# Reordering the end of attention and the routing in a one-core cross-attention and expert kernel, with filler matmuls ahead of the experts

## The chip, the cores and the metric

The kernel runs on one core of one Trainium2 chip. The metric is the device time of one execution in microseconds (us). A change of about 1% (2.3 us) is what a measurement of this kernel can tell from no change.

## What is computed

The reference is two blocks on x (1024 rows of 128) and a context of 6404 rows of 128. Cut to what matters:

```python
def xattn(c, q, ...):                         # c = layernorm(x), q = context
    cq = einsum('bcd,bqd,d->bcq', c, q, w_cq) + b_cq
    s = (c @ w_c + b_c)[:, :, None] + (q @ w_q + b_q)[:, None, :] + cq
    a = softmax(s, axis=2);  c2q = einsum('bcq,bqd->bcd', a, q)
    b_att = softmax(max(s, axis=2), axis=1)
    q2c = einsum('bc,bcd->bd', b_att, c)[:, None, :]
    return concat([c, c2q, c * c2q, c * q2c]) @ W_l.T + b_l
def ffn(x, ...):                              # 8 experts, one chosen per row by argmax
    expert_id = argmax(x @ wr + br)
    return gelu(x @ w1[e] + b1[e]) @ w2[e] + b2[e]    # e = expert_id of the row
x = x + xattn(layernorm(x), ctx, ...)
x = x + ffn(layernorm(x), ...)
```

## The kernel before

The 1024 rows are 8 tiles of 128 (t = 0 to 7); T = 8, TA = 7, H = 4. The context is cut into 7 pieces of up to 1024 (NG = 7; the last has 260 columns, three tiles). For each row tile TensorE makes the scores, VectorE (DVE) takes them out of PSUM with their maximum (L798), ScalarE (ACT) does the exponential (L649) and its rounded float16 part (L664), and DVE (`low`, L815) or, for a few pieces, GpSimd (POOL, L531) makes the float16 remainder. SyncE (SP) then transposes each piece by DMA, strictly in order of pieces (L391), and TensorE's `weighted(t, e)` (L1073, L1075) multiplies the transposed piece e of tile t with the context. In the last tile (t = 7) POOL makes the remainders of pieces 1, 3 and 5, DVE those of 0, 2, 4 and 6.

Behind the last scores there is a long tail with an order written out by hand on each engine; an engine takes its own instructions in order, and waits are semaphores:

- `attended(t)` (DVE, L820 to L828) divides the sums of tile t by the softmax total; it waits for the last `weighted(t, 6)`. `turn_a(g)` (TensorE, L1117) transposes the result of a group of tiles, `transposed(g)` (DVE, L870, L871) copies it out and multiplies it by c.
- `mean_context` (TensorE, L1174, L1176) makes q2c; DVE turns it into the weights `wc2` (L899 to L902).
- `linear_a(g)` (L1132, L1134) and `linear_c(g)` (L1141) are the output linear layer; `residual(g)` (DVE, L879) adds x; `statistics`, `variance`, `deviation` are the second layernorm, with one square root on ACT (L620); x2n is its result (L916 on DVE for tiles 0 to 3, L681 on ACT for tiles 4 to 6).
- Tiles 0 to 6 are dispatched: `turn_x2` (TensorE, L1153), `router` (L1160, L1166), `best` (DVE, L928 to L933), the one-hot choice (L939, `chosen_ready`), the ranks (TensorE, L1210 to L1217), the position arithmetic (DVE, L945 to L955, `pos_ready`). POOL then scatters the 7 tiles of rows into DRAM (L600), and SP reads them back sorted by expert in batches (L447). SP has filled that DRAM area with empty rows before (L429).
- The last tile (7) is not dispatched: it goes through all 8 experts as blocks 0 to 7, with a mask. Its chain is `residual(2)`, `statistics`, `normalise`, a transpose (L1221), its copies (L690, L964), then the first `up`.
- The experts are 22 blocks: 8 for the last tile, 14 of dispatched rows. `up(b)` (L1265 to L1268) makes the hidden layer, `down(b)` (L1279 to L1285) the output; a loop runs `up(b + 2)` before `down(b)`. At b = 6 and later `turn(g)` (L1239) transposes the batches of sorted rows. `up(8)` waits for `xT_low` of the first batch (DVE L975, behind an ACT copy). POOL scatters each block to the output (L606).

Of the kernel before, what the change touches and what calls it, by code (L numbers as in the profile page):

```python
# [30 lines left out]
P = 128  # L31


def build(nc, x, ctxT, w3, b3, wlT, b_l, wr, br, w1, b1, w2, b2, out):
# [45 lines left out]
    with es:  # L80
# [637 lines left out]
        def _(dve):  # L718
# [98 lines left out]
            def attended(t):  # L817

                acc = psA[t % 2]
                nc.vector.tensor_reduce(out=Ls[:, :], in_=Lp[:, t * NG:(t + 1) * NG], axis=AX.X,  # L820
                                        op=ALU.add).then_inc(o_small, 1)
                dve.wait_ge(o_small, 3 * t + 1)
                nc.vector.reciprocal(Li[:, :], Ls[:, :]).then_inc(o_small, 1)
                dve.wait_ge(o_small, 3 * t + 2)
                dve.wait_ge(pv_done, (t + 1) * NG)
                nc.vector.tensor_scalar(otmp[:, :], acc[:, 0:D], Li[:, :], None, ALU.mult).then_inc(o_small, 1)
                dve.wait_ge(o_small, 3 * t + 3)
                nc.vector.scalar_tensor_tensor(out=a_sb[:, t * D:(t + 1) * D], in0=acc[:, D:2 * D],  # L828
                                               scalar=Li[:, :], in1=otmp[:, :], op0=ALU.mult,
                                               op1=ALU.add).then_inc(o_out, 1)  # L830
# [42 lines left out]
            def residual(g):  # L873
# [21 lines left out]
            transposed(1)  # L895
            attended(T - 2)

# [5 lines left out]
                                           op0=ALU.mult, op1=ALU.add).then_inc(wc2_ready, 1)  # L903
            low(T - 1, 4)
            transposed(2)
            residual(0)
            low(T - 1, 6)
            statistics(x1, 0, H)
            residual(1)
            statistics(x1, H, TA)  # L910
            variance(0, TA)
            deviation(0, TA)
# [5 lines left out]
            attended(T - 1)  # L918
            transposed(3)

# [19 lines left out]

            residual(2)
            statistics(x1, TA, T)

# [11 lines left out]
            nc.vector.tensor_copy(pos[:, :], posf[:, :]).then_inc(pos_ready, 1)  # L955

            normalise(x1, x2n, TA, T, x2n_ready)

# [69 lines left out]
        def _(pe):  # L1028
# [141 lines left out]
            def mean_context():  # L1170

                pe.wait_ge(eb_ready, 1)
                for t in range(T):
# [3 lines left out]
                    .then_inc(q2c_in_psum, 1)  # L1177

            weighted(T - 2, 2)
            pe.wait_ge(scores_out, T * NG)  # L1180
# [7 lines left out]
                .then_inc(top_in_psum, 1)  # L1188
            weighted(T - 2, 4)
            weighted(T - 2, 5)  # L1190
            linear_a(0)
            weighted(T - 2, 6)
            mean_context()
            linear_a(1)
            weighted(T - 1, 0)
            turn_a(2)
            linear_c(0)
            weighted(T - 1, 1)
            linear_a(2)
            linear_c(1)  # L1200
            for e in range(2, NG):
                weighted(T - 1, e)
            turn_x2()
            turn_a(3)
            router()
            linear_a(3)
            linear_c(2)

# [7 lines left out]
            for t in range(TA):  # L1216
                last = nc.tensor.matmul(count_psum, ones16[:, :], oneh[:, t, :], start=(t == 0), stop=(t == TA - 1))  # L1217
            last.then_inc(ranks_in_psum, 1)

            pe.wait_ge(x2n_ready, H + 1)  # L1220
# [75 lines left out]
            for b in range(NBLK):  # L1296
                if b == E - 2:
                    turn(0)
                for g, (s0, _) in enumerate(BATCHES):
                    if g >= 2 and b == E + s0 - 5:  # L1300
                        turn(g)
                if b + 2 < NBLK:
                    up(b + 2)
                if b == E - 2:
                    turn(1)
                down(b)

# [30 lines left out]
```

## Time and profile before

| | us |
|---|---|
| median of 3 runs | 233.35 |
| the runs | 233.14, 234.91, 233.35 |
| the profiled execution's time | 234.7 |
| its span in the trace | 233.0 |

Busy shares of the span: TensorE 86%, DVE 77%, ACT 68%, POOL 54%. Stages of the profiled span: attention up to about 150 us, the tail of attention with the routing up to 181.4 us, the experts up to about 227 us, and the last scatters of the output. The profiled execution's own time is 1.7 us over its span, and 1.35 us over the median of the runs.

### The profile page before, as it was taken

What the parts mean: (1) busy time and instruction counts of PE and PEld (TensorE: products, weight loads), DVE (VectorE), ACT (ScalarE), POOL (GpSimd) and SP (SyncE); (2) the same over time, 40 slices, a digit from 0 to 9 for tenths busy, and PEclk for the clock granted to TensorE, in tenths of its full rate; (3) what the DMA queues carried; (4) which work ended last, traced back from release to release, by engine and by line L of the source; (5) the groups of instructions that cost most, each with busy time, mean ns of one, the idle gap of its engine ahead of it and who ended that gap; (6) DMA issues with size and microseconds to landing.
All of it is one profiled execution on the core that took longest, in us unless ns stands there. A gap on an engine that the chain in (4) does not pass through costs nothing.

```text
span 233.0 us, 5011 instructions
## 1 busy us (share of the span) xinstructions
PE 200.8 (86%) x1837; PEld 151.4 (65%) x1837; DVE 180.4 (77%) x395; ACT 157.9 (68%) x249; POOL 126.6 (54%) x177
## 2 busy tenths in 40 slices
PE   0289969999999999979989999899992899799970
PEld 0133436776866777746656777699981899789960
DVE  2999797697998997997995999957848437567770
ACT  2752899399399698699596799789332355766630
POOL 3695819708906808958608957655302730027783
PEclk9999985799999999999999999999996569999995
DMA  6999979979999999999989999989991559999100
GB/s 208 381 259 258 221 239 249 225 192 191 232 180 227 260 220 271 231 200 240 230 207 274 207 249 230 211 180 212 234 284 47 191 191 314 366 370 344 43 21 0
DMA packets 142958, 51.78 MB, mean 222 GB/s; under 512 B 121172, under 2 KB 140773, under 8 KB 142934
## 3 DMA queue, kind: packets, MB, share of 16 engines
q1 hardware_dynamic: 142000, 50.08, 92.8%
q0 software_dynamic: 784, 1.38, 1.7%
q8 instruction: 14, 0.23, 0.4%
q14 instruction: 10, 0.08, 0.1%
q10 hardware_dynamic: 150, 0.00, 0.0%
HBM read 10.74 MB, written 3.75 MB: 62 GB/s over the span
## 4 chain that ended last, share of the span: by engine, by line
PE 41%; DVE 23%; issue 13%; DMA 11%; POOL 6%; ACT 4%; SPq 1%; POOLq 0%; DVEq 0%; ACTq 0%
DMA PT<-Phl 9%; DVE S L798 6%; PE psX L1073 6%; PE psS L1055 5%; PE psS L1053 5%; PE psS L1054 5%; POOL out_x L606 5%; PE psO L1073 4%; DVE Phl L815 4%; PE psX L1075 3%; ACT S L649 3%; PE psO L1075 2%; PE psS L1279 2%; DMA S<-in_x 2%; PE psX L1084 2%
## 5 line engine op out<-in xcount | busy, mean ns | idle before, releaser
L649 ACT ACTIVATE S<-S,negb 128x1024 f32<-128x1024 f32 x48 | 55.0, 1145 | 17.5 <-DVE negb L806 17.5
L798 DVE TENSOR_SCALAR_CACHE_REDUCE S<-psS 128x1024 f32<-128x1024 f32 x48 | 58.2, 1216 | 9.9 <-PE psS L1055 9.8
L815 DVE TENSOR_TENSOR Phl<-S,Phl 128x1024 f16<-128x1024 f32 x38 | 51.5, 1354 | 5.3 <-ACT Phl L664 5.2
L531 POOL TENSOR_TENSOR Phl<-S,Phl 128x256 f16<-128x256 f32 x40 | 26.4, 691 | 52.2 <-ACT Phl L664 52.2
L664 ACT CAST Phl<-S 128x1024 f16<-128x1024 f32 x48 | 50.2, 1045 | 5.6 <-DMA PT<-Phl 4.2
L1053 PE MATMUL psS<-qT,gh 128*128 128x512 f16 x96 | 37.6, 392 | 5.6 <-DVE gl L776 3.0
L1073 PE MATMUL psO<-qn,PT 128*128 128x256 f16 x204 | 37.7, 279 | 0.7 <-DMA PT<-Phl 0.7
L1073 PE MATMUL psX<-qn,PT 128*128 128x256 f16 x204 | 36.4, 273 | 2.0 <-DMA PT<-Phl 2.0
L1055 PE MATMUL psS<-qT,gl 128*128 128x512 f16 x96 | 37.7, 393 | 0.0
L1054 PE MATMUL psS<-qT,gh 128*128 128x512 f16 x96 | 37.7, 393 | 0.0
L1075 PE MATMUL psO<-qn,PT 128*128 128x128 f16 x204 | 36.2, 223 | 0.0
L1075 PE MATMUL psX<-qn,PT 128*128 128x128 f16 x204 | 35.0, 219 | 0.0
L606 POOL DMA_INDIRECT out_x<-stageT,S x14 | 16.8, 1198 | 24.3 <-DVE stageT L1006 18.5
L1073 PEld LDWEIGHTS psO<-qn,PT 128*128 128x128 f16 x204 | 20.4, 100 | 6.5 <-DMA PT<-Phl 1.9
L1073 PEld LDWEIGHTS psX<-qn,PT 128*128 128x128 f16 x204 | 20.0, 98 | 6.7 <-DMA PT<-Phl 2.7
L708 ACT ACTIVATE Phl<-psS 128x512 f16<-128x512 f32 x22 | 13.1, 597 | 15.4 <-PE psS L1268 8.7
L1075 PEld LDWEIGHTS psO<-qn,PT 128*128 128x128 f16 x204 | 20.4, 100 | 2.2 <-issue 0.3
L1075 PEld LDWEIGHTS psX<-qn,PT 128*128 128x128 f16 x204 | 20.0, 98 | 2.1
L1053 PEld LDWEIGHTS psS<-qT,gh 128*128 128x128 f16 x96 | 9.8, 102 | 14.7 <-DVE S L798 3.5
L1055 PEld LDWEIGHTS psS<-qT,gl 128*128 128x128 f16 x96 | 9.7, 101 | 12.1 <-issue 1.4
L983 DVE TENSOR_TENSOR Phl<-Phl 128x512 f16<-128x512 f32 x22 | 15.0, 681 | 2.4 <-issue 2.4
L572 POOL TENSOR_TENSOR wp<-stageT,wp 128x256 f16<-128x256 f32 x16 | 15.2, 982 | 0.3
(239 smaller groups left out, 426.3 us busy)
## 6 DMA issues: line engine op xcount, KB each, us to landing
PT<-wp SPq DMA_DIRECT2D x8, 512.0 KB, 6.0
stageT<-in_ctxT SPq DMA_DIRECT2D x6, 512.0 KB, 7.3
qn<-wp SPq DMA_DIRECT2D x6, 512.0 KB, 6.5
wp<-in_w SPq DMA_DIRECT2D x4, 512.0 KB, 4.8
stageT<-in_w SPq DMA_DIRECT2D x4, 512.0 KB, 4.8
rows_by_expert<-stageT SPq DMA_DIRECT2D x4, 385.5 KB, 5.3
PT<-Phl SPq DMA_TRANSPOSE x48, 4.2
S<-rows_by_expert SPq DMA_DIRECT2D x2, 258.0 KB, 5.9
```

The lines of the kernel that those rows point to most:

```text
L531: last = nc.gpsimd.tensor_tensor(lo[:, r], slot(t, e)[:, r], hi[:, r], ALU.subtract)
L572: last = nc.gpsimd.tensor_tensor(parts[:, 1, at + a:at + a + CHUNK], src[:, a:a + CHUNK], parts[:, 0, at + a:at + a + CHUNK], ALU.subtract)
L606: pool.indirect_dma_start(out=out, out_offset=bass.IndirectOffsetOnAxis(ap=rows[:, b, 2 * D:ROW].bitcast(I32), axis=0), in_=yf[:, b, :], i ...
L649: nc.scalar.activation(slot(t, e), slot(t, e), ACT.Exp, bias=negb[:, t:t + 1], accum_out=Lp[:, t * NG + e:t * NG + e + 1]).then_inc(exp_do ...
L664: nc.scalar.copy(hi, slot(t, e)).then_inc(high_done, 1)
L798: nc.vector.tensor_scalar(out=into, in0=bank(u, n)[:, 0:into.shape[1]], scalar1=1.0 / GS, scalar2=None, op0=ALU.mult, op1=ALU.max, accum_o ...
L815: nc.vector.tensor_tensor(lo, slot(t, e), hi, ALU.subtract).then_inc(low_done, 1)
L1053: nc.tensor.matmul(dst, g_h, hi, start=True, stop=False)
L1054: nc.tensor.matmul(dst, g_h, lo, start=False, stop=False)
L1055: last = nc.tensor.matmul(dst, g_l, hi, start=False, stop=True)
L1073: nc.tensor.matmul(acc[:, 0:2 * D].rearrange("p (a d) -> p a d", a=2), PT[:, 2 * e * TW + i, :], both[:, :, i, :], start=(j == 0), stop=Fa ...
L1075: last = nc.tensor.matmul(acc[:, 0:D], PT[:, 2 * e * TW + n + i, :], both[:, 0, i, :], start=False, stop=(j == QT - 1), skip_group_check=True)
```

## The change

On DVE, `attended(6)` goes behind `wc2`; the remainders `low(7, 4)` and `low(7, 6)` go behind the statistics of the first and second group; `transposed(3)` goes from before `best` to behind the one-hot choice; `residual(2)` and the statistics of the last tile go from before the ranks to behind the positions. On TensorE the pieces of `weighted`, the linear layer and the transposes are put in another order: `turn_x2` and `router` stand ahead of the last one or two pieces of tile 7, `linear_a(3)` and `linear_c(2)` behind the ranks, and then 12 new matmuls over constant ones, 512 columns each, run whose result nobody reads (`fill(12)`). At expert block 6, `down(6)` goes ahead of `up(8)`.

```diff
--- before.py
+++ after.py
@@ -893,7 +893,6 @@
             nc.vector.tensor_scalar(nM[:, :], psS[0][:, CH:CH + 1], -1.0, None, ALU.mult).then_inc(nM_ready, 1)
             low(T - 1, 2)
             transposed(1)
-            attended(T - 2)
 
             dve.wait_ge(q2c_in_psum, 1)
             link(nc.vector.reciprocal(Bi[:, :], psS[1][:, CH:CH + 1]))
@@ -901,13 +900,14 @@
             dve.wait_ge(late_landed, 16 * NLATE)
             nc.vector.scalar_tensor_tensor(out=wc2[:, :], in0=wl[:, 3, :], scalar=q2c[:, :], in1=wl[:, 0, :],
                                            op0=ALU.mult, op1=ALU.add).then_inc(wc2_ready, 1)
-            low(T - 1, 4)
+            attended(T - 2)
             transposed(2)
             residual(0)
-            low(T - 1, 6)
             statistics(x1, 0, H)
+            low(T - 1, 4)
             residual(1)
             statistics(x1, H, TA)
+            low(T - 1, 6)
             variance(0, TA)
             deviation(0, TA)
             nc.vector.scalar_tensor_tensor(out=sc1[:, H:TA], in0=mv[:, H:TA, 0], scalar=-1.0, in1=rstd[:, H:TA],
@@ -916,7 +916,6 @@
                 nc.vector.tensor_scalar(x2n[:, t, :], x1[:, t, :], mv[:, t, 0:1], rstd[:, t:t + 1],
                                         ALU.subtract, ALU.mult).then_inc(x2n_ready, 1)
             attended(T - 1)
-            transposed(3)
 
             iob = iota_e[:, :].unsqueeze(1)
 
@@ -938,8 +937,7 @@
             io, first = best(router_psum, 0, TA)
             nc.vector.tensor_tensor(oneh[:, :, :], io, first, ALU.is_equal).then_inc(chosen_ready, 1)
 
-            residual(2)
-            statistics(x1, TA, T)
+            transposed(3)
 
             dve.wait_ge(ranks_in_psum, 1)
             link(nc.vector.tensor_tensor(more[:, :, :], count_psum.unsqueeze(2).broadcast_to([P, E, TA]),
@@ -954,6 +952,8 @@
             link(nc.vector.tensor_reduce(out=posf[:, :], in_=rank[:, :, :], axis=AX.X, op=ALU.add))
             nc.vector.tensor_copy(pos[:, :], posf[:, :]).then_inc(pos_ready, 1)
 
+            residual(2)
+            statistics(x1, TA, T)
             normalise(x1, x2n, TA, T, x2n_ready)
 
             link(nc.vector.scalar_tensor_tensor(out=eblk[:, :], in0=nblk[:, :], scalar=float(P), in1=sblk[:, :],
@@ -1176,6 +1176,14 @@
                 nc.tensor.matmul(psS[1][:, CH:CH + 1], ones[:, :], es1[:, :], start=True, stop=True)\
                     .then_inc(q2c_in_psum, 1)
 
+            filler = ones[:, :].bitcast(F16)
+
+            def fill(n):
+
+                for _ in range(n):
+                    nc.tensor.matmul(psS[2][:, 0:CH], filler[:, 0:P],
+                                     filler.unsqueeze(1).broadcast_to([P, 2, 2 * P]), start=True, stop=True)
+
             weighted(T - 2, 2)
             pe.wait_ge(scores_out, T * NG)
             turn_a(0)
@@ -1187,24 +1195,23 @@
             nc.tensor.matmul(psS[0][:, CH:CH + 1], ones[0:1, :], m2[:, :], start=True, stop=True)\
                 .then_inc(top_in_psum, 1)
             weighted(T - 2, 4)
+            linear_a(0)
             weighted(T - 2, 5)
-            linear_a(0)
+            mean_context()
             weighted(T - 2, 6)
-            mean_context()
             linear_a(1)
+            linear_c(0)
+            turn_a(2)
             weighted(T - 1, 0)
-            turn_a(2)
-            linear_c(0)
-            weighted(T - 1, 1)
             linear_a(2)
             linear_c(1)
-            for e in range(2, NG):
+            for e in range(1, NG - 2):
                 weighted(T - 1, e)
             turn_x2()
+            weighted(T - 1, NG - 2)
+            router()
+            weighted(T - 1, NG - 1)
             turn_a(3)
-            router()
-            linear_a(3)
-            linear_c(2)
 
             pe.wait_ge(chosen_ready, 1)
             nc.tensor.matmul(rank_psum, before[:, :], oneh[:, :, :].rearrange("p t e -> p (t e)"),
@@ -1216,6 +1223,10 @@
             for t in range(TA):
                 last = nc.tensor.matmul(count_psum, ones16[:, :], oneh[:, t, :], start=(t == 0), stop=(t == TA - 1))
             last.then_inc(ranks_in_psum, 1)
+
+            linear_a(3)
+            linear_c(2)
+            fill(12)
 
             pe.wait_ge(x2n_ready, H + 1)
             nc.tensor.transpose(x7T_psum, x2n[:, TA, :], idf[:, :]).then_inc(x7T_in_psum, 1)
@@ -1296,6 +1307,7 @@
             for b in range(NBLK):
                 if b == E - 2:
                     turn(0)
+                    down(b)
                 for g, (s0, _) in enumerate(BATCHES):
                     if g >= 2 and b == E + s0 - 5:
                         turn(g)
@@ -1303,7 +1315,8 @@
                     up(b + 2)
                 if b == E - 2:
                     turn(1)
-                down(b)
+                else:
+                    down(b)
 
 
 def kernel(**inputs):
```

## Rows read from the trace of the kernel before

**Rows 1.** Windows view, late stages: each engine's busy us, TensorE's granted clock, DMA

```profile
176.50:180.00 3.50, 0.00 (x0) 0.00 (x0) 2.82 (x16) 1.46 (x2) 0.66 (x1) 0.50 0.02 7
181.40:190.10 8.70, 8.66 (x72) 8.22 (x73) 2.59 (x12) 3.02 (x7) 5.60 (x6) 0.50 0.60 214
190.20:197.50 7.30, 7.30 (x115) 7.07 (x113) 5.40 (x14) 4.68 (x9) 0.00 (x0) 1.00 0.88 260
```

**Rows 2.** Timeline, TensorE: start, length in us, [idle before <- releaser]

```profile
156.97 1.90 PE L1174 MATMUL psS<-eb,c_sb 128*128 128x1 f32 x16
...
169.16 0.28 PE L1073 MATMUL psX<-qn,PT 128*128 128x256 f16 x1 [0.30 <-DMA PT<-Phl]
...
170.99 0.93 PE L1153 MATMUL psS<-idf,qT 128*128 128x128 f32 x7
...
172.67 1.73 PE L1166 MATMUL psS<-wrs,S 128*128 128x8 f32 x14
```

**Rows 3.** Timeline of DVE from the last tile's remainders to x2n

```profile
155.68 1.22 DVE L815 TENSOR_TENSOR Phl<-S,Phl 128x1024 f16<-128x1024 f32 x1 [2.67 <-ACT Phl L664]
...
157.61 0.15 DVE L820 TENSOR_REDUCE Ls<-Lp 128x1 f32<-128x7 f32 x1
...
158.38 0.35 DVE L828 SCALAR_TENSOR_TENSOR a_sb<-psO,Li,otmp 128x128 f32<-128x128 f32 x1
...
159.52 0.51 DVE L902 SCALAR_TENSOR_TENSOR gh<-wl,q2c 128x128 f32<-128x128 f32 x1
160.12 1.52 DVE L815 TENSOR_TENSOR Phl<-S,Phl 128x1024 f16<-128x1024 f32 x1
...
162.86 0.69 DVE L879 TENSOR_TENSOR qT<-psS,stageT 128x512 f32<-128x512 f32 x1 [0.61 <-PE psS L1141]
...
166.90 0.17 DVE L741 TENSOR_SCALAR sc<-mv 128x7 f32<-128x7 f32 x1
...
168.47 1.11 DVE L916 TENSOR_SCALAR qT<-qT,mv,rstd 128x128 f32<-128x128 f32 x4
```

**Rows 4.** SyncE's queue at the transpose of piece 5 of the last tile

```profile
165.20 1.63 SPq L391 DMA_TRANSPOSE PT<-Phl  x1
```

**Rows 5.** DMA view of that one issue: the last number is us to landing

```profile
PT<-Phl SPq DMA_TRANSPOSE x1, 3.9
```

**Rows 6.** Timeline of DVE from the router to the last tile's layernorm

```profile
174.50 0.22 DVE L928 TENSOR_REDUCE S<-psS 128x7 f32<-128x56 f32 x1 [1.40 <-PE psS L1166]
...
175.50 0.22 DVE L939 TENSOR_TENSOR S<-iota_e,S 128x56 f16<-128x56 f32 x1
175.63 0.28 DVE L879 TENSOR_TENSOR qT<-psO,stageT 128x128 f32<-128x128 f32 x1
...
176.28 0.18 DVE L735 BATCH_NORM_AGGREGATE mv<-st 128x2 f32<-128x6 f32 x1
176.50 0.22 DVE L945 TENSOR_TENSOR S<-psS,kedge 128x56 f32<-128x56 f32 x1
...
178.34 0.14 DVE L741 TENSOR_SCALAR sc<-mv 128x1 f32<-128x1 f32 x1
...
179.72 0.35 DVE L760 TENSOR_SCALAR qT<-qT,mv,rstd 128x128 f32<-128x128 f32 x1
```

**Rows 7.** Timeline of TensorE in the experts: first up, first waiting up, one down

```profile
181.44 0.27 PE L1265 MATMUL psS<-S,wp 128*128 128x128 f16 x1 [0.84 <-DVE S L964]
...
199.51 0.23 PE L1265 MATMUL psS<-S,PT 128*128 128x128 f16 x1 [1.44 <-DVE S L975]
...
200.86 0.60 PE L1279 MATMUL psS<-wp,Phl 128*128 128x256 f16 x4
...
201.57 0.22 PE L1265 MATMUL psS<-S,PT 128*128 128x128 f16 x1
```

**Rows 8.** SyncE's queue: first read-back of sorted rows

```profile
190.01 0.90 SPq L447 DMA_DIRECT2D S<-rows_by_expert  x2
```

**Rows 9.** DMA view of the first of these two issues

```profile
S<-rows_by_expert SPq DMA_DIRECT2D x1, 192.0 KB, 2.6
```

## The prediction, made before the changed kernel was run

> **What bounds the kernel now.** I read the page first: TensorE is busy 86% of the span and the granted clock is at half only in two stretches, one early and one around the start of the experts. The change touches nothing before about 151 us, so I took the windows view of the late stages, and then the timelines of TensorE and DVE through them. Three things are to be seen.
>
> First, the end of attention. TensorE waits 0.30 us for a DMA transpose at 169.16, ahead of the last two pieces of tile 7; then come the x2n transposes at 170.99 and the router matmuls, done at 174.4 [rows 2]. DVE had x2n for tiles 0 to 3 ready at 168.47 + 1.11 = 169.58 [rows 3], so `turn_x2` stood 1.4 us behind `weighted`. That is all that the new order can win there.
>
> Second, the routing. `best` starts at 174.50, the choice at 175.50, the positions at 176.50, and these end as the variance of tile 7 starts, 178.34; tile 7 is normalised at 180.07 [rows 6], and the first `up` starts at 181.44 [rows 7]. This is a chain of short DVE operations, and TensorE idles in it: none busy from 176.5 to 180 [rows 1].
>
> Third, the experts. After that idle stretch the granted clock is 0.50, which is 1.2 GHz, from 181.4 to 190.1, with TensorE busy 8.66 of 8.70 us; from 190.2 to 197.5 it is 1.00, 2.4 GHz, busy all the time [rows 1]. So the experts are bound by TensorE, and the half clock costs 8.7 / 2 = 4.35 us. There is one stall: `up(8)` waits 1.44 us [rows 7].
>
> **The change, part by part.**
>
> *(a) x2n.* In `mean_context` 0.50 us of `weighted(6, 6)` are moved behind it, so it starts 156.97 - 0.5 [rows 2] and `wc2`, done at 160.03, comes 0.5 to 0.6 us earlier. But DVE's work up to the variance at 166.90 gains `attended(6)`, 158.73 - 157.61 = 1.12 us, which now lies in DVE's wait for q2c, and which moves behind `wc2`. The idle 0.61 us before `residual(0)` [rows 3] goes; about 0.5 us comes back, because `turn_a(2)` now waits on TensorE behind `linear_c(0)` and DVE waits for it. The sum is -0.55 + 1.12 - 0.61 + 0.5 = +0.46: x2n is ready at about 170.0 in place of 169.6. Bounds: -0.3 (no new wait, and a shorter `low`) and +0.9.
>
> *(b) Piece 4 of tile 7.* `low(7, 4)` ran at 160.12 to 161.64. It now stands behind `residual(0)` and four tiles' statistics. From the new end of `wc2`, 159.45: `attended(6)` 1.12, the wait for `turn_a(2)` 0.5, `transposed(2)` 0.65, `residual(0)` 0.7, and the statistics, for which I take 1.3 of the 4.04 us between 162.86 and 166.90 [rows 3] (this stretch holds them with two residuals, `low(7, 6)` and three tiles more); the remainder starts near 163.8 and ends near 165.3. SP issues transposes in order of pieces, and piece 5, whose remainder POOL finishes at 165.2, is queued behind piece 4. One issue takes 1.63 us [rows 4] and lands 3.9 us after its start [rows 5]. So piece 4 lands at 165.3 + 3.9 = 169.2 or, as the two issues are close to each other, a little later, say 169.6; piece 5 at 167.0 + 3.9 = 170.9, where it landed at 169.1. TensorE would be ready for piece 4 near 167.4, so it idles about 2.2 us. That is hidden in part, since x2n isn't ready before 170.0, but `weighted(7, 4)`, eight times 384 columns, ends at 170.9 (a `down` has 1664 columns and takes 0.71 us [rows 7], so 3072 take 1.31 us), and `turn_x2` starts there: the same moment as before, and not 1.4 us earlier. Low bound: if the piece lands by 168.7, `turn_x2` starts with x2n, 0.9 us earlier.
>
> DVE's remainder took 1.22 us at 155.68, when POOL was idle, and 1.52 us at 160.12, beside a POOL remainder [rows 3]. Its new place is beside POOL's last remainder, so I take the longer one. The Trainium skill (SBUF — State Buffer, Who interferes with whom) says that a DVE operation with two SBUF inputs contends with a GpSimd one that reads SBUF; by that rule the move costs both engines. The trace agrees, with the 1.52 against 1.22 us.
>
> *(c) The router and the choice.* `turn_x2` takes 0.9 us, then `weighted(7, 5)` 1.3 us covers the ACT copies of x2T, then the router 2.05 us (two small ones ahead of the 1.73 [rows 2]): 170.9 + 0.85 + 1.32 + 2.05 = 175.1, against 174.4. Now the new wait: on DVE `attended(7)` still stands before `best`, and it needs `weighted(7, 6)`, which is now behind the router: 0.55 us, and then 0.75 us for its two long operations, each like the 0.35 us at 158.38 [rows 3]. `best` starts at 175.1 + 0.6 + 0.8 = 176.55 in place of 174.50: **+2.05 us** for the choice. Behind it are queued the ranks, the positions, POOL's row scatters and SP's read-backs. Bounds: +1.1 (piece 4 in time, x2n not later) and +2.6.
>
> *(d) Behind the choice.* `transposed(3)` (0.6 us) lies under the rank matmuls, whose result set the next step at 176.50 - 175.50 = 1.0 us after the choice; that is 0.1 us shorter at best. `residual(2)` and the statistics, 175.63 to 176.46 = 0.84 us [rows 6], were under the ranks and now are behind the positions, bare. So the first `up` is 5.94 - 0.1 + 0.84 = 6.7 us behind the choice, which starts at 177.55: 184.25 in place of 181.44 [rows 7], **+2.8 us**.
>
> *(e) The filler.* `linear_a(3)` and `linear_c(2)` are 0.7 us at full clock, and twelve matmuls of 512 columns, by a `down`'s 1664 columns in 0.71 us, are 2.6 us; double both at half clock. From the end of the ranks, 178.5, they reach 181.7 at full clock or 185 at half clock; the transpose of x2n, queued behind them, could start at 182.9. I expect the clock to be at half by the ranks, as it was by 176.5 [rows 1], since router, idle and ranks together are longer now. Then the filler is 6.5 us of unbroken work, which like the unbroken work before 190.1 brings the clock back, mostly before the experts start; on the way it delays the first `up` by up to 1 us, 0.25 in the middle. Credit: 4.35 - 0.25 = **-4.1 us**. Bounds: 0 (the clock is at half again or still) and -4.35. The filler writes a bank that no one reads then, and costs nothing else.
>
> That filler is needed is also what the Trainium skill says (TensorE: Matmul & The Clock Gate, Part 1): throttled is the default, activity releases it, and one kernel has different numbers of slow matmuls from execution to execution. By the second half, the 8.7 us of this execution aren't those of every one; the runs, 233.14 to 234.91 about a profiled 234.7, fit that.
>
> *(f) `down(6)` before `up(8)`.* A `down` takes 201.57 - 200.86 = 0.71 us [rows 7]. `up(8)` waits for a DVE operation which this doesn't move, so the whole `down` goes into the 1.44 us stall: **-0.7 us**; 0 if the stall is gone or the rows are late.
>
> The other moves on TensorE (linear and `weighted` pieces changing places, `turn_a(3)`) cost nothing: same instructions, under DVE's chain. From `up(8)` on all is as before, paced by TensorE.
>
> **Sum** on the profiled execution's own 234.7 us: + 2.8 - 4.1 - 0.7 = 232.7. It is 1.35 us over the median; I give the median's difference no part, because most of it lies in the length of the half-clock stretch, which this change replaces; I forecast 232.6 for the median, that is 0.3% below 233.35.
>
> **The rivals.**
>
> 1. *The forecast*: later start, warm clock. 232.6, own range 231.4 to 234.0. Chance 0.50.
>
> 2. *The cold start stays* (other side). The filler ends and about 1.2 us of idle, the transpose and 0.8 us more follow before `up(0)`; or the filler at half clock is too short. For it speaks that it took 8.7 us of nearly unbroken work to bring the clock back at 190.1, more than the filler has; against it, that this work had thin stretches (the router of tile 7 lies in it), and that a filler of 512 columns has none. Then 234.7 + 2.8 - 0.7 = 236.8. It decides from 3.3 us of remaining half-clock cost (over 6.6 us at half clock). Chance 0.16; cases between, with 3 to 6 us at half clock, give 234.2 to 235.7, chance 0.10.
>
> 3. *Attention's end is not late.* Piece 4 lands in time and x2n is no later, so the choice is at +1.1: 232.6 - 0.95 = 231.7; with a warm clock throughout, an unhindered filler and shorter waits, 230.8. For it: my +0.46 and +0.5 are small sums of guesses. Chance 0.19, nearly all of it counted as faster where the experts also gain.
>
> 4. *The rows bind.* The first sorted rows land at 190.01 + 2.6 = 192.6 [rows 8, 9]; all of it goes with the positions, +1.95: 194.6. `turn(0)` stands at 198.07 - 1.6 = 196.5 after the change. So 1.9 us of slack; if scatters or read-backs slow by more than that, the time is about 233.5. Chance 0.05.
>
> **The numbers.** Over 1% faster is under 231.0, over 1% slower over 235.7. Faster: rival 3, 0.19. Slower: rival 2, 0.16. Within 1%: 0.65. Range 230.8 to 235.8: from rival 3's end up to where the cold start decides.
>
> **What would show it.** Right: a TensorE idle before `weighted(7, 4)`, released by a DMA; `best` behind `attended(7)` at about 176.5; the first `up` near 184 to 185; granted clock 1.00 in nearly all of the first eight blocks; no 1.44 us stall before `up(8)` without a `down` in it. Wrong: `up(0)` earlier than 183.5, or a clock of 0.5 for over 4 us behind it, or a wait of `turn(0)` for rows.

## The result, and the profile of the changed kernel

The changed kernel took 237.0 us in the median of 4 runs (236.15 to 237.42), the kernel before 233.78 (233.14 to 234.91): ratio 1.0114, 95% interval 1.0073 to 1.0154. I had forecast 232.6 with a range up to 235.8. It is 1.1% slower, the interval leaves out 1, and the time is outside the range.

The profiled execution of the changed kernel took 236.77 us, its span is 235.04 (233.0 before). Below, times are also given from the start of the DVE operation that makes `nM`, the last thing both kernels do in the same order (L893 in both). Windows view of the changed kernel (engines' busy us, then the granted clock, DMA share, GB/s), which answers to [rows 1]:

```profile
178.00:184.80 6.80, 5.68 (x29) 3.26 (x30) 5.64 (x28) 1.63 (x3) 1.44 (x2) 0.50 0.27 84
186.90:198.90 12.00, 12.00 (x185) 11.60 (x186) 8.00 (x25) 7.64 (x15) 3.87 (x4) 1.00 0.57 194
```

The filler did what it was expected to: the granted clock was 0.50 from 178.0 to 184.8, under the ranks and the filler, and the first blocks ran at 1.00 throughout. Timeline of DVE, which answers to [rows 3] and [rows 6]:

```profile
155.00 0.15 DVE L893 TENSOR_SCALAR nM<-psS 128x1 f32<-128x1 f32 x1
...
165.89 1.65 DVE L815 TENSOR_TENSOR Phl<-S,Phl 128x1024 f16<-128x1024 f32 x1
...
171.01 1.11 DVE L916 TENSOR_SCALAR qT<-qT,mv,rstd 128x128 f32<-128x128 f32 x4
...
177.68 0.35 DVE L826 TENSOR_SCALAR otmp<-psX,Li 128x128 f32<-128x128 f32 x1 [5.30 <-PE psX L1075]
...
179.32 0.22 DVE L938 TENSOR_TENSOR S<-iota_e,S 128x56 f16<-128x56 f32 x1
```

Timeline of POOL, the remainder that runs beside DVE's at 165.89:

```profile
164.53 3.54 POOL L531 TENSOR_TENSOR Phl<-S,Phl 128x256 f16<-128x256 f32 x4 [1.82 <-ACT Phl L664]
```

Timeline of TensorE, which answers to [rows 2] and [rows 7]:

```profile
171.47 0.28 PE L1073 MATMUL psX<-qn,PT 128*128 128x256 f16 x1 [1.81 <-DMA PT<-Phl]
...
172.80 0.93 PE L1153 MATMUL psS<-idf,qT 128*128 128x128 f32 x7
...
181.57 4.37 PE L1184 MATMUL psS<-ones 128*128 128x512 f16 x12
185.77 0.27 PE L1232 MATMUL psO<-idf,qT 128*128 128x128 f32 x1
186.89 0.22 PE L1276 MATMUL psS<-S,wp 128*128 128x128 f16 x1 [0.84 <-DVE S L964]
...
208.89 0.66 PE L1250 MATMUL psX<-idf,S 128*128 128x128 f32 x4 [1.17 <-DMA S<-rows_by_expert]
```

TensorE waits 1.81 us for piece 4's transpose; `attended(7)` (L826) waits for the last piece behind the router, and the choice (L938) is 24.32 us behind `nM`, against 22.64 before; the first `up` is 31.88 us behind it, against 28.58. The last row is new: the third turn of sorted rows (the third `turn(g)`) waits for its DMA. In the kernel before, the same turn waited for nothing:

```profile
206.87 0.61 PE L1239 MATMUL psX<-idf,S 128*128 128x128 f32 x4
```

SP's first read-back, which answers to [rows 8]:

```profile
195.71 0.90 SPq L447 DMA_DIRECT2D S<-rows_by_expert  x2
```

That is 40.7 us behind `nM` in place of 37.15: 3.55 us later. The positions account for 1.6 us of it (done at 27.14 us behind `nM`, 25.57 before), and the scatters' landing for the rest: from the end of POOL's last scatter to the read-back it is 3.82 us here and 1.48 before.

The table holds the eleven profiles that the argument uses most; the names are explained with the experiments.

| us behind `nM` (start of it in the span) | choice | first up | first read-back | third turn | end of span |
|---|---|---|---|---|---|
| before (152.86) | 22.64 | 28.58 | 37.15 | 54.01 | 80.11 |
| before_again (153.16) | 22.63 | 28.57 | 37.79 | 52.48 | 78.59 |
| changed (155.01) | 24.32 | 31.88 | 40.70 | 53.88 | 80.03 |
| after_again (153.02) | 24.25 | 30.84 | 40.01 | 53.69 | 81.48 |
| after_third (154.72) | 24.28 | 30.90 | 39.03 | 56.20 | 82.50 |
| after_nofill (153.65) | 24.24 | 30.92 | 39.12 | 55.28 | 81.39 |
| after_w6_first (153.94) | 23.59 | 31.40 | 39.40 | 54.60 | 82.46 |
| after_low4_w6 (155.95) | 22.16 | 28.85 | 37.15 | 54.15 | 80.54 |
| before_fill (155.07) | 22.57 | 28.36 | 37.57 | 50.96 | 77.11 |
| before_fill_fourth (153.98) | 22.62 | 28.50 | 38.07 | 51.97 | 78.12 |
| before_fill_third (154.16) | 22.73 | 28.76 | 39.23 | 55.08 | 81.19 |

### The profile page after: what moved, and what is told of

It is laid out like the page before. It is cut to its first block, busy times and chain, and to the rows that moved or that the text cites. A ratio compares the mean times of both kernels' runs of the same rounds, so it can differ in the third digit from the quotient of the medians.

```text
span 235.0 us, 5034 instructions
## 1 busy us (share of the span) xinstructions
PE 202.7 (86%) x1849; PEld 149.8 (64%) x1849; DVE 180.1 (77%) x395; ACT 157.7 (67%) x249; POOL 126.9 (54%) x177
## 4 chain that ended last, share of the span: by engine, by line
PE 44%; DVE 20%; DMA 14%; issue 9%; POOL 5%; SPq 4%; ACT 1%; POOLq 0%; DVEq 0%
DMA PT<-Phl 7%; PE psO L1073 6%; PE psS L1053 6%; PE psX L1073 6%; PE psS L1055 6%; PE psS L1054 6%; DVE S L798 6%; DVE Phl L815 6%; DMA S<-rows_by_expert 3%; PE psO L1075 3%; PE psX L1075 3%; POOL rows_by_expert L600 3%; POOL out_x L606 2%; DMA rows_by_expert<-qT,S 2%; DMA S<-in_x 2%
## 5 line engine op out<-in xcount | busy, mean ns | idle before, releaser
L531 POOL TENSOR_TENSOR Phl<-S,Phl 128x256 f16<-128x256 f32 x40 | 27.1, 710 | 51.8 <-ACT Phl L664 51.8
L708 ACT ACTIVATE Phl<-psS 128x512 f16<-128x512 f32 x22 | 13.2, 599 | 10.7 <-PE psS L1279 10.7
L1055 PEld LDWEIGHTS psS<-qT,gl 128*128 128x128 f16 x96 | 9.7, 101 | 12.1 <-issue 1.4
L572 POOL TENSOR_TENSOR wp<-wp 128x256 f16<-128x256 f32 x16 | 15.4, 989 | 0.3
```

The lines of the kernel that those rows point to most:

```text
L531: last = nc.gpsimd.tensor_tensor(lo[:, r], slot(t, e)[:, r], hi[:, r], ALU.subtract)
L572: last = nc.gpsimd.tensor_tensor(parts[:, 1, at + a:at + a + CHUNK], src[:, a:a + CHUNK], parts[:, 0, at + a:at + a + CHUNK], ALU.subtract)
L1055: last = nc.tensor.matmul(dst, g_l, hi, start=False, stop=True)
```

## The experiments

The runs came in five groups. Each group ran on one chip beside the kernel before (the expectations call a group a call); ratios are to the kernel before of the same group, with 95% intervals. The groups' chips differ, and that matters below. Theories of the first group: H, the first 150 us vary by themselves; P, the changed program is slower there; F, the filler earns its 3 to 4 us; R, the sorted rows cap what it earns. Later groups use letters that their expectations explain.

**First group: both kernels again, and the filler taken from one and given to the other.**

> The kernel before, once more, for a second profile of it. Anchor: the start of the DVE operation that makes nM (the end of the untouched head), 152.86 us in the first profile of before and 155.00 us in that of the changed kernel; the rest of the span was 80.1 and 80.0 us. Theory H (the head varies from execution to execution, whatever the program): this profile's anchor lies anywhere from 152.5 to 155.5. Theory P (the changed program has a slower head by itself): the anchor is again 152.5 to 153.3. The rest of the span is 78.5 to 80.1 us by both, shorter where the half-clock stretch at the start of the experts is shorter than the 8.7 us of the first profile. Time ratio 1.000 to within 0.3%.

> The changed kernel, once more. Theory H: its anchor lies anywhere from 152.5 to 155.5 us, and the ratio to before comes from the rest of the span alone, which is then 80.0 us against about 79 us in a typical execution of before: ratio 1.003 to 1.006. Theory P: anchor again 154.5 to 155.5 and ratio about 1.011.

```diff
 after_nofill (from the changed kernel)
-            fill(12)
```

> The changed kernel without the twelve filler matmuls. Theory F (the filler is what brings the clock back before the experts and so earns 3 to 4 us): the first up starts about 1.1 us earlier, but at half clock for 6 to 9 us; the sorted rows bind less. Time 1 to 2.5 us above the changed kernel. Theory R (the sorted rows bind anyway, so a warm start is worth little): the filler gained at most what the rows leave; time within 0.7 us of the changed kernel, on either side.

```diff
 before_fill (from the kernel before; fill as the changed kernel has it)
             last.then_inc(ranks_in_psum, 1)
+            fill(12)
```

> The kernel before with the same twelve filler matmuls behind the ranks and nothing else changed. Theory F: the clock is at full speed for nearly all of the first eight blocks and the time falls by 2.5 to 3.7 us (ratio 0.984 to 0.989), the rest of the 4.35 us going to waits for sorted rows at the third and fourth batch. Theory R: the rows bind from the first batch on, and the time falls by less than 1 us (ratio over 0.996).

Measured: before_again 1.0014 (0.9977 to 1.005); after_again 1.010 (1.0062 to 1.0138); after_nofill 1.011 (1.0058 to 1.0162); before_fill 0.9954 (0.992 to 0.9989).

*The head.* `nM` starts at 153.02 us in after_again, at 153.16 in before_again, at 155.07 in before_fill, whose program is that of before up to there. Over all twenty profiles its mean is 153.9 us, for kernels built from the old order and from the new one alike. So the head goes by theory H: the 2.15 us that the first pair of profiles shows ahead of 155 us (152.86 against 155.01) don't come from the change, though they are the whole difference of that pair. The ratio of 1.010, from 12 runs of the changed kernel beside 29 of the kernel before, is the measure of the change. It is above the 1.003 to 1.006 that I had expected by H: the rest of the kernel loses more than I thought.

*The tail*, from before_again and after_again, the same chip, 78.59 against 81.48 us. (The medians of these two differ by 2.4 us; this pair of executions is somewhat further apart.) Windows of before_again, then of after_again:

```profile
181.80:187.20 5.40, 5.40 (x46) 5.18 (x46) 1.94 (x9) 1.97 (x5) 4.03 (x5) 0.50 0.69 246
```

```profile
183.80:195.90 12.10, 12.04 (x186) 11.68 (x187) 8.05 (x25) 7.70 (x15) 5.02 (x5) 1.00 0.58 193
208.10:211.40 3.30, 3.30 (x29) 2.97 (x27) 1.68 (x4) 1.08 (x2) 0.00 (x0) 0.50 1.09 363
```

Third turn of after_again in TensorE's timeline:

```profile
206.71 0.66 PE L1250 MATMUL psX<-idf,S 128*128 128x128 f32 x4 [2.02 <-DMA S<-rows_by_expert]
```

First up +2.27; from there to the first turn 14.63 against 12.08, -2.55 (this execution of before had 5.6 us at half clock, and not 8.7); first to third turn 9.28 against 10.77, +1.49, which is +2.02 of waiting for rows, -0.72 of `down(6)` and 0.2 of smaller things; from the third turn to the end 26.11 against 27.79, +1.68, which is the half clock from 208.1 to 211.4: TensorE had just waited 2.02 us for the rows. (Waits of 1.17 and 1.92 us there, in the first profile of the changed kernel and in before_fill_fourth below, were not followed by one.) The sum is +2.89 us.

*Where the filler's gain goes.* before_fill starts its first up where before does and has no half clock at all from there; up to the first turn it gains 2.5 us on before_again. At the third turn it waits:

```profile
206.03 0.66 PE L1248 MATMUL psX<-idf,S 128*128 128x128 f32 x4 [1.05 <-DMA S<-rows_by_expert]
```

In the four profiles where that turn waits for rows and SP's order is that of before (changed, after_again, before_fill, before_fill_fourth) it starts 13.2 to 13.9 us behind SP's first read-back, whenever TensorE gets there. before stood 3.6 us above the lowest of these, before_again 1.5. So a warm start is worth about that much and no more, and a later read-back of a kernel that waits there is paid in full. That is R rather than F: the time fell by 0.46%, about 1.1 us, and not by the 1.1 to 1.6% of F. (I had put R's limit at 1 us and the first batch; it is the third that binds.)

And after_nofill, with 7.9 us at half clock, is as fast as the changed kernel (1.011 against 1.010, each to within some 0.5%). Its third turn comes 55.28 us behind `nM` and waits for nothing. With the filler it comes at 53.69 (after_again) and 53.88 (changed), 1.4 to 1.6 us earlier, for the warm start's 3.7 us, and after_again loses even these again to its second half-clock stretch. In the runs the filler buys the changed kernel nothing that can be told from noise.

Windows view of after_nofill:

```profile
184.60:192.50 7.90, 7.90 (x65) 7.43 (x66) 2.28 (x10) 3.38 (x7) 4.63 (x5) 0.50 0.66 233
```

**Second group: single parts.**

```diff
 before_down6: down(6) ahead of up(8), in the kernel before
 after_w6_first (from the changed kernel)
-            router()
             weighted(T - 1, NG - 1)
+            router()
 after_rows_early (from the changed kernel)
+            block_rows(2, 0, D, rows_landed)
             fetch(4)
             fetch(5)
-            block_rows(2, 0, D, rows_landed)
 (and block_rows(3, 0, D, rows_landed) ahead of fetch(8))
 before_fill_down6_rows: filler, down(6) and this order in the kernel before
```

> The kernel before with down(6) ahead of up(8) and nothing else changed. Theory D (TensorE paces the experts from their start): the 0.7 us of the down go into the stall of 1.44 us and the time falls by 0.6 to 0.8 us, ratio 0.997. Theory R (the third batch of sorted rows, turned 13.2 us after SP's first read-back, binds in many executions): in the two profiles of before the third turn stood 3.6 and 1.4 us above that, so by R also the 0.7 us are had, unless the clock comes back early. Ratio 0.997 to 0.999 by R.

> The changed kernel with weighted(7, 6) ahead of the router, so that attended(7) on DVE runs under the router and no longer between the router and best. Theory R: what sets the end is SP's first read-back of sorted rows, which follows the positions. The choice comes 0.6 to 0.8 us earlier, the first read-back too, and the time falls by as much: 0.7 us, ratio to before about 1.007. If the empty rows' landing holds back the scatters instead (theory E: the scatters waited for it in three profiles), the choice comes earlier but the first scatter doesn't, and the time stays within 0.3 us of the changed kernel.

> The changed kernel with SP's read-back of the third and fourth batch of rows moved ahead of two and one weight fetches. Theory R: the third turn no longer waits (1.2 and 2.0 us in the two profiles of the changed kernel), the clock doesn't fall a second time, and the time falls by 1.2 to 2.5 us, ratio to before 1.000 to 1.005. Theory D (the rows' wait is only where the engine would lose the time anyway, at a later block's weights): less than 0.5 us.

> The kernel before with the filler, down(6) ahead of up(8), and the earlier read-back of the third and fourth batch. Theory R: the filler's warm start, worth 0.46% alone, is no longer capped by the rows: the first up to the third turn takes 21.3 us (22.6 with the filler alone), time 2.3 to 3.3 us under before, ratio 0.986 to 0.990. Theory D: the weights of the dispatched blocks bind instead, ratio 0.993 to 0.996.

Measured: 0.9998 (0.9955 to 1.004), 1.006 (1.0016 to 1.0104), 1.013 (1.0085 to 1.0176), 1.0063 (1.0026 to 1.01).

before_down6: its own part is seen in the trace, first to third turn 8.57 us in place of 9.29; the run's time can't tell 0.3%. after_w6_first: the choice is 0.7 us earlier, as expected. Its ratio points the same way, but the changed kernel itself did not run on this chip and the intervals overlap, so the gain in time isn't shown. The last two were clear misses. No turn waits for rows (after_rows_early's third stands at 208.12 with no wait), but TensorE got there late, because of gaps that no engine releases; so these two don't test whether earlier rows lift R's cap. after_w6_first has such gaps too. None of the six profiles of the first pair and the first group has them. before_fill shows them when it is run again in later groups; timeline of TensorE in before_fill_third:

```profile
187.83 0.22 PE L1277 MATMUL psS<-stageT 128*128 128x128 f16 x1 [0.50 <-issue]
...
188.54 0.22 PE L1275 MATMUL psS<-S,wp 128*128 128x128 f16 x1 [0.43 <-issue]
...
189.27 0.22 PE L1276 MATMUL psS<-S,wp 128*128 128x128 f16 x1 [0.52 <-issue]
...
190.67 0.22 PE L1276 MATMUL psS<-S,wp 128*128 128x128 f16 x1 [1.01 <-issue]
```

Each gap is followed by two to ten weight loads and matmuls and then the next gap; they come to 2.0 to 3.2 us of idle TensorE in all. Windows view of the same stretch, in before_fill_third and then in before_fill, which has none:

```profile
187.00:191.00 4.00, 1.54 (x20) 0.91 (x18) 0.11 (x1) 1.29 (x3) 1.94 (x3) 1.00 0.77 275
```

```profile
187.00:191.00 4.00, 4.00 (x65) 3.88 (x63) 2.70 (x9) 3.04 (x7) 3.39 (x3) 1.00 0.80 286
```

The idle time is not their whole price. In seven of the nine profiles that have them with 12 filler matmuls, the granted clock then falls to half for 3.4 us, as here in before_fill_third:

```profile
191.40:194.80 3.40, 3.28 (x27) 2.74 (x26) 1.92 (x5) 2.00 (x5) 0.00 (x0) 0.50 0.08 10
```

From the first up to the first turn takes 12.1 to 12.2 us in the four profiles with the filler, without gaps and with SP's old order, 14.6 and 14.9 in the two where the clock stays up behind the gaps (after_w6_first, after_rows_early), and 16.7 to 17.8 in the seven where it falls. So the gaps cost 2.5 to 5.7 us, as much as the filler gains there (2.5 and 4.1 us against the two profiles of before) or more.

**Third group: rows or gaps, and the two late steps of the order undone together.**

```diff
 before_fill_again: before_fill once more
 before_fill_rows: before_fill with the rows' order of after_rows_early
 before_fill_late (from before_fill)
-            for b in range(FIRST):
-                fetch(b)
             sp.reg_load(expert_reg[FIRST:NB], bexp[0:1, FIRST:NB])
             ...
             block_rows(0, 0, D, rows_landed)
+            for b in range(FIRST):
+                fetch(b)
             block_rows(1, 0, D, rows_landed)
 after_low4_w6 (from the changed kernel): after_w6_first, and on DVE
             attended(T - 2)
+            low(T - 1, 4)
             transposed(2)
             residual(0)
             statistics(x1, 0, H)
-            low(T - 1, 4)
```

> The kernel before with the filler alone, once more. Theory R: 0.3 to 0.7% under before again (0.46% in the first call), with the third turn waiting about 1 us for its rows. Theory I (TensorE, once it is fast at the start of the experts, runs into gaps of about 1 us that no engine releases, as it did for 2 to 3 us between 185 and 191 us in three of the four profiles of the second call, and in none of the first): where such gaps show in the profile, the gain is less, down to none.

> The kernel before with the filler and with the read-back of the third and fourth batch of rows issued ahead of two and one weight fetches. Theory R: from the first up to the third turn 21.4 us in place of 22.6, no wait of a turn for rows, and 0.8 to 1.2 us under the kernel with the filler alone. Theory W (the reordering takes from the weights what it gives the rows): no more than 0.3 us under it, with waits of up for a fetched weight.

> The kernel before with the filler, and the first two weight fetches (0.5 MB each, which kept the DMA engines full from 185 to 189 us) issued behind the first read-back of rows instead of ahead of the last scatters. Theory I with its cause in these transfers (they delay TensorE's own supply of instructions): no gap of TensorE without a releaser before 190 us, in a call where the other filler kernels show them. Against it: the gaps stay. Either way the first read-back starts 0.5 to 1 us earlier, as the scatters have the DMA engines for themselves, and the third turn moves with what is queued ahead of its rows, 0 to 2 us later.

> The changed kernel with low(7, 4) back ahead of transposed(2) and weighted(7, 6) ahead of the router. By the steps of the prediction the choice was late by what these two cost: piece 4's wait (1.8 us of TensorE idle in the changed kernel, of which about 0.5 to 1 us reach the router) and attended(7) ahead of best (0.75 us). Expected: the choice 22.6 to 23.1 us behind nM (24.3 in the changed kernel, 22.6 before), no DMA wait ahead of piece 4, and the time 1.2 to 1.7 us under the changed kernel, ratio to before 1.002 to 1.005. If the time stays above 1.008, what costs is not the choice but what is behind it (tile 7's statistics behind the positions, and the filler's delay of x2n's transpose).

Measured: 1.0061 (1.0018 to 1.0104), 1.0055 (1.0021 to 1.009), 1.0051 (1.0002 to 1.0101), 1.0048 (1.0014 to 1.0083).

All four profiles have the gaps, 2.5 to 3.2 us, and the half clock behind them. before_fill, 0.46% faster in the first group, is 0.61% slower in this one. The gaps stay in before_fill_late, so the two fetches are not their cause. The rows' order can't be judged while TensorE is late for the third turn anyway.

after_low4_w6 shows what the order had cost at the choice. Its timeline of DVE:

```profile
155.95 0.15 DVE L893 TENSOR_SCALAR nM<-psS 128x1 f32<-128x1 f32 x1
...
163.44 1.28 DVE L815 TENSOR_TENSOR Phl<-S,Phl 128x1024 f16<-128x1024 f32 x1
...
175.11 0.35 DVE L826 TENSOR_SCALAR otmp<-psX,Li 128x128 f32<-128x128 f32 x1 [2.70 <-PE psX L1075]
...
177.11 0.21 DVE L927 TENSOR_REDUCE S<-psS 128x7 f32<-128x56 f32 x1 [1.27 <-PE psS L1166]
...
178.11 0.22 DVE L938 TENSOR_TENSOR S<-iota_e,S 128x56 f16<-128x56 f32 x1
```

`attended(7)` now runs under the router, and `best` waits for the router alone. The choice is 22.16 us behind `nM`: 2.1 us earlier than in the changed kernel and 0.5 earlier than before. The first up comes 2 us earlier than in the changed kernel. With these two undone the new order is no longer a loss: 1.0048 beside 1.0061 for before with the filler, same chip, both with the gaps. The changed kernel as it was did not run in this group, so the gain in time over it, 1.010 to 1.0048, is one across chips.

**Fourth group: is the gap tied to the stream of instructions?**

```diff
 after_third, before_fill_third: the changed kernel and before_fill once more
 before_fill72, after_fill72: 72 filler matmuls of 128 columns for 12 of 512
```

> The changed kernel, a third time, as the control of this call: ratio to before 1.010. If TensorE's gaps without a releaser between the first up and the first turn show in this call (theory S: TensorE's supply of instructions, at a fixed place of its stream), up to 3 us of them stand here too, and the ratio is 1.012 to 1.018; if not, the third turn waits 1 to 2 us for rows instead.

> The kernel before with the filler of 12 matmuls, a third time. Without gaps in this call: ratio 0.994 to 0.997 as in the first call. With gaps: 1.004 to 1.007 as in the third, and they start at the same place in TensorE's instruction stream as in the other profiles with gaps: 120 to 130 recorded weight loads and matmuls behind the first up.

> The kernel before with a filler of 72 matmuls of 128 columns in place of 12 of 512. Its stream has 60 more weight loads and 60 more matmuls ahead of the first up. Theory S (gaps at a fixed place in the stream of instructions): gaps, if this call shows any, start 0 to 15 records behind the first up and not 120 to 130, or fall into the filler where they cost nothing. Theory P (gaps at a fixed place in the program, whatever the stream ahead): they start 120 to 130 records behind the first up as before. The filler ends about 1.5 us later, close to the moment x2n of tile 7 is ready, so the first up is 0 to 1 us later.

> The changed kernel with the same longer filler. Theory S as in the run before. The filler, begun at half clock, delays the transpose of x2n of tile 7: it needs 4 us at full and 8 us at half clock from the end of linear_c(2), so the first up comes 1 to 3 us later than in the changed kernel, and the time is 0 to 2 us above the changed kernel unless the gaps it avoids pay for that.

Measured: 1.0159 (1.0099 to 1.0219), 1.0105 (1.0051 to 1.0159), 1.0181 (1.0119 to 1.0244), 1.030 (1.0247 to 1.0353).

before_fill_third lies above the 1.004 to 1.007 that I had expected of it with gaps; its interval takes them in. before_fill72's first up comes 2.85 us later than before_fill_third's, where I had expected 0 to 1. I counted TensorE's recorded instructions (weight loads, matmuls and some 30 semaphore instructions) from the start of the program to the first gap. With 12 filler matmuls the first up is number 2595, and the gaps start between 2699 and 2723 in all profiles that have them. With 72 it is number 2715, and the gap starts at 2713, between the transpose of x2n and the first up, in both kernels. before_down6, without filler and with its first up at number 2571, has its small gap at 2712 too. Timeline of TensorE in before_fill72:

```profile
183.22 0.28 PE L1229 MATMUL psO<-idf,qT 128*128 128x128 f32 x1
186.06 0.22 PE L1273 MATMUL psS<-S,wp 128*128 128x128 f16 x1 [2.57 <-DVE S L964]
```

DVE is named there, but it waited for ACT, and ACT for TensorE's signal on a transpose that had ended at 183.5:

```profile
185.26 0.27 ACT L690 CAST S<-psO 128x128 f16<-128x128 f32 x1 [3.40 <-remote]
```

So the gap is at a fixed place of TensorE's stream and not of the program: theory S. It costs there too: from the transpose to the first up it is 2.84 us in place of 1.11 (before_fill_third), 1.7 us more, where I had hoped that it would fall where it costs nothing. In after_fill72 the gap at this place is 3.40 us long, and its first up comes 36.20 us behind `nM`, 5.3 us later than in after_third, where I had expected 1 to 3; at 1.030 it is the slowest of all.

**Fifth group: is it the traffic?**

```diff
 before_fill_fourth: before_fill once more
 before_fill_quiet (from before_fill_late), on POOL
             pool.wait_ge(pos_ready, 1)
+            pool.wait_ge(y_ready, 4)
             for t in range(TA):
```

> The kernel before with the filler, as the control of this call: it tells whether this chip shows TensorE's gaps without a releaser, 0 or 2 to 3 us of them between the first up and the first turn.

> The same with POOL's row scatters held back until the fourth expert block is done, and the first two weight fetches behind the first read-back, so that next to no DMA runs from 182 to 190 us. The rows come some 10 us later, so the total is several us longer and says nothing. Theory C (the scatters' or the fetches' traffic holds up TensorE's supply of instructions): no gap without a releaser in this stretch, where the control shows some. Theory N (it is not the traffic): the gaps stay, 120 to 145 records behind the first up. If the control shows none, the run decides nothing.

Measured: before_fill_fourth 0.9926 (0.9887 to 0.9965), no gap, and a third turn that waits 1.92 us for rows. before_fill_quiet (251.64 and 247.69 us, as its rows come some 14 us later) has no gap either, with 2 GB/s of traffic from 186.1 to 195.0, but as its control has none, it decides nothing.

```profile
186.10:195.00 8.90, 8.90 (x139) 8.59 (x139) 5.53 (x18) 6.02 (x13) 0.00 (x0) 1.00 0.01 2
```

## Why the prediction was wrong

Every sign that I had named for being right is in the changed kernel's profile, once the 2.15 us of its later head are taken off, and none of those for being wrong; the time was outside the range all the same. The sum took a credit for a warm clock in full, and the rows that TensorE then has to wait for pass on only a part of it.

| part, us | forecast | before to changed | before_again to after_again |
|---|---|---|---|
| the head, up to `nM` | 0 | +2.15 | -0.14 |
| first up: (a) to (d) | +2.8 | +3.30 | +2.27 |
| first up to first turn: (e) | -4.1 | -4.05 | -2.55 |
| first to third turn: (f) | -0.7 | +0.62 | +1.49 |
| third turn to the end | 0 | +0.05 | +1.68 |
| sum from `nM` on | -2.0 | -0.08 | +2.89 |

- *(a) x2n* later by 0.46: it starts 16.0 us behind `nM` where it was 15.61, +0.4. Right.
- *(b) Piece 4.* TensorE's idle was 1.81 us against 2.2 forecast. Right. The remainder took 1.65 us and POOL's beside it 3.54 (2.79 before), more than the 1.52 that I took for DVE's.
- *(c) The choice.* Forecast +2.05, measured +1.6 to +1.7, by the two mechanisms named: undoing both gave 2.1 us.
- *(d) The first up.* Forecast +2.8; +3.3, +2.3, +2.3 in three profiles. In the first of them the filler ran mostly at half clock and held up the transpose of x2n by 1.1 us (x2n was ready at 184.69, the transpose started at 185.77), where I had put 0.25 into (e); without the filler (after_nofill) the first up comes at the same 30.9 us as in the other two.
- *(e) The filler* is the step that failed. The clock came back as forecast, and in the first profile the first blocks gained 4.05 us. But the credit of 4.1 us was put into the sum whole. It is capped by rival 4, which I gave 0.05 after working out its slack at the first turn of rows. The 1.9 us of slack was itself misread: 198.07 is the end of that turn, which starts at 197.58, so it was 1.4. And the turn that binds is the third, 13.2 us or more behind the first read-back, whose slack I did not work out. I had the read-back later by 1.95 us; in the first two profiles it was later by 3.5 and 2.2, because beside the positions' 1.6 and 1.5 the scatters took longer to land (3.8 and 2.9 us behind the last of them, for 1.5 and 1.7). The wait cost 1.2 and 2.0 us, and in one profile a second half-clock stretch of 3.4 us cost 1.7 us more. What the runs show in place of -4.1 us: -1.1 us for the filler in the kernel before (0.9954), and nothing that can be told from noise in the changed kernel. Beyond that, executions of the old order have 5.6 to 8.7 us at half clock (8.7, 5.6 and 7.0 in before, before_again and before_down6); I noted that they differ and still took the longest as the credit.
- *(f) down(6)*: 0.72 us between first and third turn, as forecast. On the path where the rows wait, it buys nothing.
- Rival 4's price, 233.5, was too low for the same reason: it left out that the whole end of the kernel hangs on the third turn (it follows by 26.1 to 26.2 us in twelve of the twenty profiles, and never by less), and what the clock does behind the wait.
- Rival 2 had the right sign by another mechanism: the start was not cold.
- The gaps were in no rival, and neither profile of before shows them. In after_third they are 2.4 us, with 3.4 us at half clock behind them, and its ratio is 1.016 against 1.010 without them; the two intervals overlap.

So what makes the kernel slower is what I had priced rightly, the later first up and the rows queued behind the later choice, and what failed is the credit set against it. Part of the distance to 237.0 us is chance: by the ratio of the first group, 1.010, the time would be 235.7, at the edge of my range and still on the wrong side of 233.35.

What stays open: that the rows cap the gain is read from the traces and from before_fill and after_nofill; the direct test, earlier rows, fell to the gaps each time. And what holds TensorE up at that place. It is not the two weight fetches; whether the row scatters have a part wasn't decided. A queue that the page calls "instruction" moves one packet of 16 KB in this stretch, but in before_fill_third it starts at 191.21 us, when the last gap is over, so those gaps aren't waits for this packet (in before_fill_again it moves from 189.6 to 191.1, during the last of them). Nor is it shown why some chips show the gaps and others not: three of the groups had them in each kernel with the filler, two groups in none. And no version beat the kernel before on all of them: before_fill was at 0.9926 and 0.9954 on two chips, at 1.0061 and 1.0105 on two others.

## What to carry to other kernels

When a stage is sped up, work out the slack of every later arrival that it meets, the third as well as the first, from the release of that arrival's own chain; the smallest slack is the cap of the gain. An instruction moved behind another engine's work must be followed to who waits for it: here one `attended` left ahead of `best`, while the `weighted` that it needs went behind the router, put 0.7 us on the longest chain, and moving that three-tile `weighted` took it off again. And a difference between two profiles should be split at the last point where both programs are the same before any of it is laid to the change.

## What the runs showed of the hardware

- TensorE can be held up for 2 to 3 us in gaps of 0.2 to 1.2 us that no engine releases (in one piece of up to 3.4 us with the longer filler), at a fixed place of its instruction stream (number 2699 to 2723 from the start), on three of the five groups' chips and not on the other two. With 12 filler matmuls they end at 188.9 to 192.8 us of the span. Who comes to the place late loses little: before_down6, at half clock until 188.4, got there at 189.4 and lost 0.24 us, and 0.23 us a little later.
- Such gaps were followed by 3.4 us at a granted clock of 0.50 in seven of nine profiles.
- The untouched first part took 151.6 to 156.3 us from execution to execution, independent of the program's later part.
- The row scatters can wait for the DMA that writes the empty rows: in before_again, although the positions were done at 178.7, the first scatter started at 180.44, released by that DMA.
- From the end of POOL's last row scatter to SP's first read-back it took 1.5 to 4.1 us in nineteen profiles and 6.3 in after_fill72.
